# Gated delta-net layer: gram products and decay blocks eight steps ahead, q/k projection nine, nine block buffers, block transfers merged

## The chip, the cores and the metric

One core of one Trainium2 chip (trn2) runs the whole program. The metric is device time in microseconds, the median over runs. All times below are microseconds unless marked ns.

## What is computed

The program is a two-layer transformer on `x` of shape 4 x 256 x 256 (batch `b`, time, width), each layer an attention part and a feed-forward part with adaptive layer norm. The change touches the attention part of the first layer alone, a gated delta rule with 16 key heads and 32 value heads of width 128:

```python
q, k, v = silu(causal_conv4(h @ W_qkvz))      # z is split off before the convolution
q, k = l2norm(q) / sqrt(128), l2norm(k)
def step(S, (q_t, k_t, v_t, a_t, b_t)):       # over 256 times, per batch and value head
    S = S * a_t
    S = S + k_t x ((v_t - S.k_t) * b_t)
    return S, S.q_t
o = rmsnorm(o * silu(z)) * norm_weight        # then @ W_out, gate and residual
```

The recurrence is computed in chunks of 128 times. In each chunk the products k.k and q.k (the gram products), weighted with the decays, give triangular matrices; the lower triangular one has to be inverted.

## The kernel before

**The loop.** The loop over key heads `kh` = 0 to 15 with batches `b` = 0 to 3 inside has 64 steps. All of its order is written out by hand: `pe_step`, `act_step`, `dve_step` and `pool_step` say what TensorE (PE), ScalarE (ACT), VectorE (DVE) and GpSimd (POOL) do in step (kh, b), in this order, and one list of transfers on SyncE (SP) runs beside them. Engines meet at semaphores alone, and each executes its own list in order. Counting the steps as g = 4 kh + b, three kinds of work run ahead of the step that uses them:

- q and k are projected, convolved and squashed eight steps ahead (`LEAD_QK` = 8): `pe_qk`, `act_tap0`, `dve_tap`, `act_silu_qk`.
- The gram products (`pe_gram0`, `pe_gram1`), the decays as scans (`dve_scan`, L843, L846) and their product, the decay blocks `BP` (`dve_scales`, `dve_bp`, L892), are made seven steps ahead (`LEAD_GRAM` = 7). `BP0` and `BP1` hold four batches each, so eight blocks.
- v and z are projected three steps ahead (`LEAD_VZ` = 3).

What runs ahead is done before the loop for the first steps (lists `lead_qk`, `lead_gram`, `lead_taps`, `lead_bp`), and is absent in the last ones.

**The inverses.** The 32 x 32 diagonal blocks of the triangular matrices (64 of them for a head, all batches) go from `BP` to a scratch in DRAM (`sp_blocks_in`, L1076, four transfers for each batch) and from there, one block to a partition, into `Dm` (`sp_blocks_turn`, L1085: eight transfers, for batches 0 to 2 and then for batch 3). POOL inverts them by 31 substitution steps of two instructions (`pool_inverse`, L1023 and L1026) into `Tn`; ACT transposes `Tn` into `Tt` in two halves (`act_turn`, L718, in steps b = 2 and b = 3). `sp_blocks_out` (L1097) writes both to DRAM and `sp_blocks_read` (L1107 for `U`, L1112 for `UT`) brings them back in matrix layout, first for batches 0 and 1, then for 2 and 3. `pe_merge` (L391 to L400, with `act_merge` after each of its four stages) puts the blocks together to inverses of 128 x 128 for two batches in step b = 0 and for the other two in b = 1.

During head kh, POOL inverts the blocks of head kh + 1. `SPLIT` says which of the 31 substitution steps lie ahead of which `pool_ro`:

```python
SPLIT = ((0, 7), (7, 19), (19, 26), (26, BLK - 1))
```

`pool_ro` (L998, a power of four numbers in a partition) is needed at once: `act_ss` (L693) gives the sums of squares of a step's output, `pool_ro` the root, `act_ogn` (L701) the scaled output, `pe_ot` (L444) its transpose, and `pe_f` (L454) the output projection. For b = 0 and b = 1, ACT does all of that in the following step: in `act_step` of (kh, 1), `act_ss` and `act_ogn` of (kh, 0) stand ahead of the first `act_merge`, and in `pe_step` of (kh, 1) `pe_ot` stands ahead of the second `pe_merge` stage.

A step solves with the inverse (`pe_solve`, L420, evicted by `act_y`, L664, twice a step), and multiplies into the output (`pe_o`, L433, L435). In `act_step` of b = 3 the order is the second `act_y`, `act_ots`, and then the second half of `act_turn` for head kh + 1.

Of the kernel before, what the change touches and what calls it, by code (L numbers as in the profile page):

```python
# [23 lines left out]
P = 128  # L24
# [17 lines left out]
MODS = 6  # L42


def build(nc, x_d, wqkvz_d, wba_d, convw_d, dtb_d, alog_d, nw_d, wout_d, wg_d, sg_d, wu_d, su_d, wd_d, sd_d,
# [26 lines left out]
    with outer:  # L72
# [140 lines left out]
        with ExitStack() as s1:  # L213
# [12 lines left out]
            nrm = sb("nrm", [P, B, 4], ctx=s1)  # L226
# [8 lines left out]
            BP = [BP0, sb("BP1", [P, B, 6 * R, P], ctx=s1)]  # L235
            Dm = sb("Dm", [SLOTS, BLK, BLK], ctx=s1)
            Tn = sb("Tn", [SLOTS, BLK, BLK], ctx=s1)
            Tt = sb("Tt", [SLOTS, BLK, BLK], ctx=s1)
# [17 lines left out]
            hact += [BP[1][:].rearrange("p b z t -> p (b z t)")[:, b * 1536:(b + 1) * 1536].rearrange("p (m t) -> p m t", m=HT) for b in range(2)]  # L256

            craw = sb("craw", [B, 2, D], ctx=s1)
            csil = sb("csil", [P, 2, KC, B], ctx=s1)
            wba = sb("wba", [P, KC, NVH * 2], ctx=s1)  # L260
            dtb = sb("dtb", [P, NVH], ctx=s1)
            alog = sb("alog", [P, NVH], ctx=s1)
            ea = sb("ea", [P, NVH], ctx=s1)

            wmod = BP[1][:].rearrange("p b z t -> p (b z t)").rearrange("p (l k n) -> p l k n", l=2, k=KC)
            gx, gn, gu, gw, gl, gd = (Vs[:].rearrange("p b c h d -> p (b c h d)")[:, i * NT * NVH:(i + 1) * NT * NVH]
                                      .rearrange("p (t h) -> p t h", t=NT) for i in range(6))
            alpT = Tt[0:NVH].rearrange("s j i -> s (j i)")
# [16 lines left out]
            LEAD_QK, LEAD_GRAM, LEAD_VZ = 2 * B, 2 * B - 1, 3  # L285
# [79 lines left out]
            def block_of(p, b, h, x, c, i):  # L365

                if c == 0:
                    return BP[p][:, b, (0 if x else 4 * R) + 2 * h + i, :]
                return BP[p][:, b, 2 * R + 2 * h + 1 - x, :]

            def pe_merge(kh, p, g, stage):

                n = 2 * kh + g
                if stage == 0:
                    wait(nc.tensor, "u_zero", 1)
                    wait(nc.tensor, f"t_in0{g}", (kh + 1) * 48)
                    wait(nc.tensor, "og", at(kh, g, 2))
                else:
                    if stage == 1:
                        wait(nc.tensor, f"t_in1{g}", (kh + 1) * 64)  # L380
                    wait(nc.tensor, "u_evac", n * 6 + (1, 4, 5)[stage - 1])
                for i in range(2):
                    b = 2 * g + i
                    for m in range(NC * R):
                        c, h = divmod(m, R)
                        s = i * NC * R + m
                        low = block_of(p, b, h, 1, c, c)
# [15 lines left out]
            def pe_solve(kh, p, b, n):  # L403
# [9 lines left out]
                for h in range(R):  # L413
                    if n == 0:
                        lhs, rhs = UT[:, b, h, :], Vs[:, b, 0, h, :]
                    elif n == 1:
                        lhs, rhs = block_of(p, b, h, 1, 0, 1), Y[:, 0, h, :]
                    else:
                        lhs, rhs = UT[:, b, R + h, :], R2[:, h, :]
# [3 lines left out]
            def pe_o(kh, p, b, c):  # L423
# [7 lines left out]
                for h in range(R):  # L431
                    o = bO[:, (c * R + h) * P:(c * R + h + 1) * P]
                    last = nc.tensor.matmul(o, block_of(p, b, h, 0, 0, c), Y[:, 0, h, :], start=True, stop=(c == 0))  # L433
                    if c == 1:
                        last = nc.tensor.matmul(o, block_of(p, b, h, 0, 1, 1), Y[:, 1, h, :], start=False, stop=True)  # L435
# [432 lines left out]
            def dve_scales(kh, p, b):  # L868
                i = b % 2
                wait(nc.vector, "gram", at(kh, b, 1, 1))  # L870
                wait(nc.vector, "vpow", kh)
                nc.vector.tensor_scalar(nrm[:, b], bG2[:, 256:260], 1e-6, None, ALU.add).then_inc(sem("nrm"), 1)
                wait(nc.vector, "nrm", at(kh, b, 1, 1))
                nc.vector.reciprocal(rcn[i][:], nrm[:, b, 2:4]).then_inc(sem("rcn"), 1)
# [5 lines left out]
            def dve_bp(kh, p, b, c):  # L880
# [4 lines left out]
                for h in range(R):  # L885
                    if c == 0:
                        dst = BP[p][:, b].rearrange("p (z n) t -> p z (n t)", z=3)[:, 0:3:2, 2 * h * P:2 * (h + 1) * P]
                        g, e = bG1[:].rearrange("p (x t) -> p x t", x=2), E1[:, h, :].unsqueeze(1).broadcast_to([P, 2, T])
                    else:
                        dst = BP[p][:, b, 2 * R + 2 * h:2 * R + 2 * (h + 1), :]  # L890
# [99 lines left out]
            def pool_vpow(kh, p):  # L990
                wait(nc.gpsimd, "nrm", (kh + 1) * B)
                wait(nc.gpsimd, "og", (kh - 1) * B * 2)
                nc.gpsimd.tensor_tensor(vsc[p][:], nrm[:], npow[:].unsqueeze(1).broadcast_to([P, B, 4]), ALU.pow).then_inc(sem("vpow"), 1)
# [7 lines left out]
            SPLIT = ((0, 7), (7, 19), (19, 26), (26, BLK - 1))  # L1001
            LAST_SPLIT = ((0, 6), (6, 14), (14, 21), (21, BLK - 1))
# [13 lines left out]
            def pool_inverse(kh, lo, hi):  # L1016

                if lo == 0 and hi > 0:
                    wait(nc.gpsimd, "blk_in", (kh + 1) * 16 * 2 * NBLK)
# [48 lines left out]
            PER_B = NC * R  # L1068

            def sp_blocks_in(kh, b):  # L1070

                wait(nc.sync, "bp", at(kh, b, 4, 4))
                wait(nc.sync, "blk_in", kh * 16 * 2 * NBLK)
                for n in range(NBLK):
                    r = slice(n * BLK, (n + 1) * BLK)
                    nc.sync.dma_start(blkin_dr[n, b].rearrange("c h j i -> j (c h) i"),  # L1076
                                      BP[kh % 2][r, b, 0:4 * R:2, r]).then_inc(sem(f"blk_dr{b}"), 16)

            def sp_blocks_turn(kh, lo, hi):
                for b in range(lo, hi):  # L1080
                    wait(nc.sync, f"blk_dr{b}", (kh + 1) * 16 * NBLK)
                wait(nc.sync, "t_step", kh * NTS)
                for n in range(NBLK):
                    s = slice((n * B + lo) * PER_B, (n * B + hi) * PER_B)
                    nc.sync.dma_start(Dm[s].rearrange("s j i -> s (j i)"),  # L1085
                                      blkin_dr[n, lo:hi].rearrange("b c h j i -> (b c h) (j i)")).then_inc(sem("blk_in"), 16)

            def sp_blocks_out(kh):

                wait(nc.sync, "t_step", (kh + 1) * NTS)  # L1090
                for i, (dr, src) in enumerate(((tinv_dr, Tn), (ttin_dr, Tt))):
                    if i == 1:
                        wait(nc.sync, "t_turned", 2 * (kh + 1))
                    for g in range(2):
                        wait(nc.sync, f"t_in{i}{g}", kh * (48, 64)[i])
# [4 lines left out]
            def sp_blocks_read(kh, g):  # L1100
                bs = slice(2 * g, 2 * g + 2)
                for b in range(2 * g, 2 * g + 2):
                    wait(nc.sync, "y", at(kh - 1, b, 2, 2))
# [905 lines left out]
```

## Time and profile before

| | |
|---|---|
| runs of the program | 1272.46 median, 1269.07 to 1273.2 (3 runs) |
| the profiled execution: span from first to last instruction | 1270.6 |
| busy, share of the span | PE 92%, DVE 72%, ACT 65%, POOL 59% |
| POOL's `vpow` (L993), mean of 16 | 2.9 |
| its mean granted TensorE clock, share of full speed | 0.961 |
| DMA | 143430 packets, 72.82 MB; 116744 packets are under 512 B |

The profiled execution is known by its span; its own time outside the span is not given, and the median of the runs is 1.9 over the span. An engine's busy time counts instructions, not waits. "DMA a<-b" is a transfer, listed under SPq where it is issued; the time shown there is that of the issue. The column "PEclk" of a stretch is the granted TensorE clock (1.00 is 2.4 GHz, 0.50 is 1.2 GHz).

### The profile page before, as it was taken

Reading aid. Unit: us, or ns where it says so; the run is one execution under the profiler, and the core shown is the slowest. Engines: PE = TensorE matmul, PEld = TensorE weight load, DVE = VectorE, ACT = ScalarE, POOL = GpSimd, SP = SyncE. Lnnn points to the kernel's source line nnn. Section 1 sums busy time; section 2 is a strip of 40 time slices with the busy share of each in tenths; the row PEclk is TensorE's granted clock in tenths of the full one; section 3 lists DMA queues with packets and bytes.
Section 4 is the critical chain, followed back from the end, with each engine's and each line's share of the span. In section 5 each row is a group of like instructions: output and inputs, shape, how many; then the busy total and the mean of one; then the engine's idle time right before and its main releaser. Section 6 shows DMA issues by size and latency. Waiting matters only on the chain. (4 is left out here: it accounts for less than half of the span.)

```text
span 1270.6 us, 30469 instructions
## 1 busy us (share of the span) xinstructions
PE 1168.6 (92%) x10744; PEld 1002.5 (79%) x10744; DVE 914.6 (72%) x2304; ACT 831.6 (65%) x2289; POOL 751.5 (59%) x1187
## 2 busy tenths in 40 slices
PE   7787998999999999999999999999998688998986
PEld 6687887888888888888888888888887577776754
DVE  6786787788879797878888888879793414337764
ACT  6334776777777676777777777777675556218973
POOL 3275758586867777776858586858676601104211
PEclk9776999999999999999999999999998979999988
DMA  5212134314040313121222314040214130002000
GB/s 177 64 55 51 66 73 44 83 34 111 7 112 19 99 31 87 37 80 40 80 45 73 65 52 111 6 113 14 62 29 129 25 108 1 1 1 72 2 10 25
DMA packets 143430, 72.82 MB, mean 57 GB/s; under 512 B 116744, under 2 KB 132624, under 8 KB 141360
## 3 DMA queue, kind: packets, MB, share of 16 engines
q1 hardware_dynamic: 143280, 70.89, 22.5%
q8 instruction: 86, 1.41, 0.5%
q14 instruction: 64, 0.52, 0.1%
HBM read 57.06 MB, written 13.78 MB: 56 GB/s over the span
## 5 line engine op out<-in xcount | busy, mean ns | idle before, releaser
L1023 POOL TENSOR_TENSOR tmp<-Dm,Tn 64x31 f32<-64x31 f32 (+15 forms) x496 | 260.5, 525 | 104.0 <-DMA Dm<-blk_in_scratch 69.9
L1026 POOL TENSOR_TENSOR Tn<-Tn,tmp 64x31 f32<-64x31 f32 (+15 forms) x496 | 291.3, 587 | 38.8
L832 DVE SCALAR_TENSOR_TENSOR cv<-bank,cw,cv 128x255 f32<-128x255 f32 (+2 forms) x384 | 155.2, 473 | 145.0 <-ACT cv L631 144.8
L832 DVE SCALAR_TENSOR_TENSOR cqk<-bank,cw,cqk 128x255 f32<-128x255 f32 (+2 forms) x384 | 155.0, 472 | 16.5 <-ACT cqk L631 16.4
L998 POOL TENSOR_TENSOR ro<-ss,mhalf 128x4 f32<-128x4 f32 x64 | 68.0, 1062 | 158.2 <-issue 97.7
L892 DVE SCALAR_TENSOR_TENSOR BP<-bank,cj,E 128x512 f32<-128x512 f32 (+1 forms) x256 | 140.4, 611 | 2.6 <-DVE cj L877 0.3
L454 PE MATMUL bank<-wo,OTs 128*128 128x256 f32 x512 | 132.1, 392 | 0.9 <-ACT OTs L724 0.9
L693 ACT ACTIVATE junk<-og 128x129 f32<-128x129 f32 x256 | 79.6, 311 | 51.6 <-issue 39.4
L701 ACT ACTIVATE ogn<-og,ro 128x128 f32<-128x128 f32 x256 | 81.9, 393 | 44.4 <-POOL ro L998 44.1
L433 PE MATMUL bank<-Y,BP 128*128 128x128 f32 x512 | 95.7, 290 | 7.4 <-ACT Y L664 6.1
L454 PEld LDWEIGHTS bank<-wo,OTs 128*128 128x128 f32 x512 | 91.3, 193 | 12.0 <-ACT OTs L724 1.0
L338 PE MATMUL bank<-hh,wvz_hi 128*128 128x256 f32 x256 | 84.2, 329 | 9.0 <-ACT hT L645 9.0
L433 PEld LDWEIGHTS bank<-Y,BP 128*128 128x128 f32 x512 | 73.0, 193 | 19.4 <-ACT Y L664 19.4
L348 PE MATMUL bank<-wvz_hi,hh 128*128 128x256 f32 x256 | 83.7, 327 | 0.9
L308 PE MATMUL bank<-hh,wqk_hi 128*128 128x256 f32 x256 | 80.4, 314 | 3.1 <-DVE cqk L832 3.1
L664 ACT ACTIVATE Y<-bank 128x256 f32<-128x256 f32 x128 | 48.9, 382 | 51.6 <-PE bank L420 50.5
L318 PE MATMUL bank<-sqk 128*128 128x512 f32 x128 | 67.9, 613 | 8.8 <-DVE BP L892 8.8
L308 PE MATMUL bank<-hh,wqk_lo 128*128 128x256 f32 x256 | 74.8, 292 | 0.0
L308 PE MATMUL bank<-hl,wqk_hi 128*128 128x256 f32 x256 | 74.6, 292 | 0.0
L338 PE MATMUL bank<-hh,wvz_lo 128*128 128x256 f32 x256 | 74.2, 290 | 0.0
L338 PE MATMUL bank<-hl,wvz_hi 128*128 128x256 f32 x256 | 74.0, 289 | 0.0
L348 PE MATMUL bank<-wvz_hi,hl 128*128 128x256 f32 x256 | 73.2, 286 | 0.0
(210 smaller groups left out, 3326.9 us busy)
## 6 DMA issues: line engine op xcount, KB each, us to landing
rvz<-in_L_attn_W_qkvz SPq DMA_DIRECT2D x16, 512.0 KB, 5.5
x<-alpha_scratch SPq DMA_DIRECT2D x8, 1024.0 KB, 6.6
alb<-alpha_scratch SPq DMA_DIRECT2D x7, 1024.0 KB, 6.3
rqk<-in_L_attn_W_qkvz SPq DMA_DIRECT2D x16, 256.0 KB, 2.6
wo<-in_L_attn_W_out SPq DMA_DIRECT2D x16, 256.0 KB, 6.2
blk_in_scratch<-BP SPq DMA_DIRECT2D x256, 16.0 KB, 1.5
tinv_scratch<-Tn SPq DMA_DIRECT2D x32, 128.0 KB, 2.2
tinv_t_scratch<-Tt SPq DMA_DIRECT2D x32, 128.0 KB, 2.2
```

Source lines behind the costliest of these rows:

```text
L308: last = nc.tensor.matmul(bQK[:, t * T:(t + 1) * T], wqk[p][w][:, k, t * DK:(t + 1) * DK], h[:, k, b * T:(b + 1) * T], start=(k + n == 0), ...
L338: last = nc.tensor.matmul(bV[:, t * T:(t + 1) * T], wvz[p][w][:, k, t * DK:(t + 1) * DK], h[:, k, b * T:(b + 1) * T], start=(k + n == 0), ...
L348: last = nc.tensor.matmul(bZ[:, c * 256:(c + 1) * 256], h[:, k, b * T + c * P:b * T + (c + 1) * P], wvz[p][w][:, k, R * DK:2 * R * DK], st ...
L433: last = nc.tensor.matmul(o, block_of(p, b, h, 0, 0, c), Y[:, 0, h, :], start=True, stop=(c == 0))
L454: last = nc.tensor.matmul(bF[:, c * D:(c + 1) * D], OTs[:, h, c, :], wo[p][:, h, :], start=(h == 0), stop=(h == R - 1))
L693: nc.scalar.activation(junk[:], og[b % 2][:, c, h, :], ACT.Square, accum_out=ss[b % 2][:, n:n + 1]).then_inc(sem("ss"), 1)
L701: nc.scalar.activation(ogn[:, c, h, :], og[b % 2][:, c, h, 0:DK], ACT.Copy, scale=ro[b % 2][:, n:n + 1]).then_inc(sem("ogn"), 1)
L832: nc.vector.scalar_tensor_tensor(d, bk[:, t * T:(t + 1) * T - s], cw[p][:, first + t, TAPS - 1 - s:TAPS - s], d, ALU.mult, ALU.add).then_i ...
L892: nc.vector.scalar_tensor_tensor(dst, g, cj[i][:, c, h:h + 1], e, ALU.mult, ALU.mult).then_inc(sem("bp"), 1)
L998: nc.gpsimd.tensor_tensor(ro[b % 2][:], ss[b % 2][:], mhalf[:, 0:4], ALU.pow).then_inc(sem("ro"), 1)
L1023: pool_step_done(nc.gpsimd.tensor_tensor(t, Dm[:, j, j + 1:BLK].unsqueeze(2).broadcast_to([SLOTS, r, c]), Tn[:, j, 0:c].unsqueeze(1).broad ...
L1026: pool_step_done(nc.gpsimd.tensor_tensor(Tn[:, j + 1:BLK, 0:c], Tn[:, j + 1:BLK, 0:c], t, ALU.subtract), kh * NTS + 2 * j + 4)
```

## The change

Steps and buffers: q/k nine steps ahead, gram products and blocks eight, so that one more q/k step and one more gram step lie ahead of the loop. `BP0` holds four blocks and `BP1` five, used in turn. Before the loop, the split of head 2's q/k weights moves ahead of the ninth q/k step. `nrm` gets a second buffer. `Dm` and `Tt` become the halves of one tensor (partitions 0 to 63 and 64 to 127), and some small tensors of the start move into others' space; what those compute is the same.

```diff
+RING = 2 * B + 1
+            BP1 = sb("BP1", [P, RING - B, 6 * R, P], ctx=s1)
+            def bp_of(kh, b):
+                n = (kh * B + b + RING - 1) % RING
+                return BP0[:, n] if n < B else BP1[:, n - B]
-            LEAD_QK, LEAD_GRAM, LEAD_VZ = 2 * B, 2 * B - 1, 3
+            LEAD_QK, LEAD_GRAM, LEAD_VZ = 2 * B + 1, 2 * B, 3
```

POOL: the substitution steps in three parts instead of four; the power `pool_vpow` of the next head behind `pool_ro` of b = 0, not ahead of the inverse; the start of the next inverse (`pool_inverse_start`, L1012, L1013) in b = 3 of the head before.

```diff
-            SPLIT = ((0, 7), (7, 19), (19, 26), (26, BLK - 1))
-            LAST_SPLIT = ((0, 6), (6, 14), (14, 21), (21, BLK - 1))
+            SPLIT = ((0, 15), (15, 25), (25, BLK - 1))
             def pool_step(kh, p, b):
-                if kh + 1 < NKH:
-                    if b == 0:
-                        pool_vpow(kh + 1, 1 - p)
-                        pool_inverse_start(kh + 1)
-                    pool_inverse(kh + 1, *(SPLIT if kh + 2 < NKH else LAST_SPLIT)[b])
+                if b < len(SPLIT) and kh + 1 < NKH:
+                    pool_inverse(kh + 1, *SPLIT[b])
+                if b == B - 1 and kh + 2 < NKH:
+                    pool_inverse_start(kh + 2)
                 pool_ro(kh, p, b)
+                if b == 0 and kh + 1 < NKH:
+                    pool_vpow(kh + 1, 1 - p)
```

SP: one transfer into `Dm` in place of eight, the inverses read for all four batches at once (three transfers for `U` and four for `UT`, twice as large, in place of six and eight), and another order of the list:

```diff
+            def sp_blocks_turn(kh):
+                for b in range(B):
                     wait(nc.sync, f"blk_dr{b}", (kh + 1) * 16 * NBLK)
                 wait(nc.sync, "t_step", kh * NTS)
+                nc.sync.dma_start(Dm.rearrange("s j i -> s (j i)"), blkin_dr.rearrange("n b c h j i -> (n b c h) (j i)")).then_inc(sem("blk_in"), 16)
+            def sp_blocks_read(kh):
+                wait(nc.sync, "y", at(kh, 0, 2))
                 wait(nc.sync, "t_out0", (kh + 1) * 32)
...
                 for kh in range(NKH - 1):
-                    sp_blocks_turn(kh + 1, 0, B - 1)
-                    sp_blocks_in(kh + 1, B - 1)
-                    sp_blocks_turn(kh + 1, B - 1, B)
-                    sp_blocks_read(kh, 1)
+                    ahead = kh + 2 < NKH
+                    if ahead:
+                        sp_blocks_in(kh + 2, 0)
                     if kh + 3 < NKH:
-                        sp_load_qk(kh + 3)
                         sp_load_alb(kh + 3)
-                    if kh + 2 < NKH:
+                    if ahead:
                         sp_load_vz(kh + 2)
                     sp_load_wo(kh + 1)
...
-                    if kh + 2 < NKH:
-                        for b in range(B - 1):
-                            sp_blocks_in(kh + 2, b)
+                    if ahead:
+                        sp_blocks_in(kh + 2, 1)
+                        sp_blocks_in(kh + 2, 2)
+                    if kh + 4 < NKH:
+                        sp_load_qk(kh + 4)
                     sp_blocks_out(kh + 1)
-                    sp_blocks_read(kh + 1, 0)
-                sp_blocks_read(NKH - 1, 1)
+                    if ahead:
+                        sp_blocks_in(kh + 2, B - 1)
+                    sp_blocks_read(kh + 1)
+                    if ahead:
+                        sp_blocks_turn(kh + 2)
```

`sp_blocks_out` is unchanged but for its semaphores: it writes `Tn`, waits until ACT has transposed both halves, and writes `Tt`. `act_step` and `pe_step` are unchanged. Ahead of the loop SP's list ends in `sp_blocks_out(0)`, `sp_blocks_read(0)`, `sp_blocks_in(1, B - 1)`, `sp_load_qk(3)`, `sp_blocks_turn(1)`.

## Rows read from the trace of the kernel before

**Rows 1.** Stretches: heads 1 to 13, head 14, head 15 (start:end, length, PE busy, PEclk, DMA, GB/s)

```profile
167.20:946.00 778.80, 753.32 (x7489) 1.00 0.26 60
946.00:1002.10 56.10, 48.45 (x493) 0.94 0.34 87
1002.10:1067.20 65.10, 50.56 (x461) 0.82 0.22 64
```

**Rows 2.** Stretches: the four steps of head 8, each to the end of its last Y

```profile
588.85:609.54 20.69, 20.06 (x221) 1.00 0.43 90
609.54:626.39 16.85, 16.57 (x200) 1.00 0.32 101
626.39:635.91 9.52, 9.07 (x69) 1.00 0.05 9
635.91:647.98 12.07, 12.04 (x89) 1.00 0.04 7
```

**Rows 3.** Who waited for whom, whole span: us in total, times, longest

```profile
POOL tmp L1023 <- DMA Dm<-blk_in_scratch: 69.9, 16, 7.5
...
ACT ogn L701 <- POOL ro L998: 44.1, 44, 2.5
```

**Rows 4.** Timeline of POOL in head 7: start, us, instruction

```profile
545.81 0.23 POOL L1023 TENSOR_TENSOR tmp<-Dm,Tn 64x31 f32<-64x31 f32 x1 [5.14 <-DMA Dm<-blk_in_scratch]
...
554.16 1.01 POOL L998 TENSOR_TENSOR ro<-ss,mhalf 128x4 f32<-128x4 f32 x1
555.15 0.51 POOL L1023 TENSOR_TENSOR tmp<-Dm,Tn 64x192 f32<-64x192 f32 x1
...
566.20 0.95 POOL L1023 TENSOR_TENSOR tmp<-Dm,Tn 64x256 f32<-64x256 f32 x1
...
582.28 0.44 POOL L1023 TENSOR_TENSOR tmp<-Dm,Tn 64x156 f32<-64x156 f32 x1
```

**Rows 5.** The second step of head 7 as a stretch

```profile
549.12:566.92 17.80, 16.83 (x200) 1.00 0.38 120
```

**Rows 6.** Timeline of ACT at the start of head 8

```profile
588.46 0.39 ACT L664 ACTIVATE Y<-bank 128x256 f32<-128x256 f32 x1
...
589.31 1.11 ACT L718 ACTIVATE Tt<-Tn 64x512 f32<-64x512 f32 x1
...
612.94 0.19 ACT L693 ACTIVATION_READ_ACCUMULATOR junk<-og 128x1 f32 x1
```

**Rows 7.** Timeline of SP's queue, same time: start of issue, us of issuing, transfer, count

```profile
586.09 1.73 SPq L1076 DMA_DIRECT2D blk_in_scratch<-BP  x4
...
590.45 0.77 SPq L1097 DMA_DIRECT2D tinv_t_scratch<-Tt  x2
591.32 1.37 SPq L1107 DMA_DIRECT2D U<-tinv_scratch  x3
593.02 1.78 SPq L1112 DMA_DIRECT2D UT<-tinv_t_scratch  x4
```

**Rows 8.** The page, part 6: KB each, us from issue to landing

```profile
rqk<-in_L_attn_W_qkvz SPq DMA_DIRECT2D x16, 256.0 KB, 2.6
```

**Rows 9.** Stretches: head 14's second step, and the part behind PE's gap

```profile
964.81:983.52 18.71, 15.31 (x177) 0.82 0.66 190
971.25:976.20 4.95, 4.95 (x61) 0.50 0.86 227
```

**Rows 10.** Timelines ahead of the loop: DVE, PE, PE

```profile
102.27 2.19 DVE L892 SCALAR_TENSOR_TENSOR BP<-bank,cj,E 128x512 f32<-128x512 f32 x4
...
104.60 1.10 PE L318 MATMUL bank<-sqk 128*128 128x512 f32 x2 [4.02 <-DVE BP L892]
...
113.79 0.23 PE L391 MATMUL bank<-U,BP 32*32 32x32 f32 x1 [1.92 <-DMA U<-tinv_scratch]
```

**Rows 11.** Timelines near the end of the loop: POOL in head 14, PE in head 15

```profile
968.88 1.01 POOL L998 TENSOR_TENSOR ro<-ss,mhalf 128x4 f32<-128x4 f32 x1
...
1011.74 0.55 PE L338 MATMUL bank<-hh,wvz_hi 128*128 128x256 f32 x1 [5.22 <-ACT hT L645]
```

More of the change, by code:

```diff
@@ L225, in build @@
             sv = [sb(f"sv{i}", [P, R, T], ctx=s1) for i in range(2)]
-            nrm = sb("nrm", [P, B, 4], ctx=s1)
+            nrm = [sb(f"nrm{p}", [P, B, 4], ctx=s1) for p in range(2)]
             ss = [sb(f"ss{i}", [P, 4], ctx=s1) for i in range(2)]
@@ L375, in pe_merge @@
                     wait(nc.tensor, "u_zero", 1)
-                    wait(nc.tensor, f"t_in0{g}", (kh + 1) * 48)
+                    wait(nc.tensor, "t_in0", (kh + 1) * 48)
                     wait(nc.tensor, "og", at(kh, g, 2))
@@ L379, in pe_merge @@
                     if stage == 1:
-                        wait(nc.tensor, f"t_in1{g}", (kh + 1) * 64)
+                        wait(nc.tensor, "t_in1", (kh + 1) * 64)
                     wait(nc.tensor, "u_evac", n * 6 + (1, 4, 5)[stage - 1])
@@ L432, in pe_o @@
                     o = bO[:, (c * R + h) * P:(c * R + h + 1) * P]
-                    last = nc.tensor.matmul(o, block_of(p, b, h, 0, 0, c), Y[:, 0, h, :], start=True, stop=(c == 0))
+                    last = nc.tensor.matmul(o, block_of(kh, b, h, 0, 0, c), Y[:, 0, h, :], start=True, stop=(c == 0))
                     if c == 1:
-                        last = nc.tensor.matmul(o, block_of(p, b, h, 0, 1, 1), Y[:, 1, h, :], start=False, stop=True)
+                        last = nc.tensor.matmul(o, block_of(kh, b, h, 0, 1, 1), Y[:, 1, h, :], start=False, stop=True)
                 last.then_inc(sem("o"), 1)
@@ L870, in dve_scales @@
                 wait(nc.vector, "gram", at(kh, b, 1, 1))
-                wait(nc.vector, "vpow", kh)
-                nc.vector.tensor_scalar(nrm[:, b], bG2[:, 256:260], 1e-6, None, ALU.add).then_inc(sem("nrm"), 1)
+                wait(nc.vector, "vpow", kh - 1)
+                nc.vector.tensor_scalar(nrm[p][:, b], bG2[:, 256:260], 1e-6, None, ALU.add).then_inc(sem("nrm"), 1)
                 wait(nc.vector, "nrm", at(kh, b, 1, 1))
-                nc.vector.reciprocal(rcn[i][:], nrm[:, b, 2:4]).then_inc(sem("rcn"), 1)
+                nc.vector.reciprocal(rcn[i][:], nrm[p][:, b, 2:4]).then_inc(sem("rcn"), 1)
                 wait(nc.vector, "rcn", at(kh, b, 1, 1))
@@ L1018, in pool_inverse @@
                 if lo == 0 and hi > 0:
-                    wait(nc.gpsimd, "blk_in", (kh + 1) * 16 * 2 * NBLK)
+                    wait(nc.gpsimd, "blk_in", (kh + 1) * 16)
                 for j in range(lo, hi):
@@ L1147, in _ @@
                     sp_blocks_in(0, b)
-                sp_blocks_turn(0, 0, B - 1)
-                sp_blocks_turn(0, B - 1, B)
+                sp_blocks_turn(0)
                 sp_load_qk(2)
@@ L1155, in _ @@
                 sp.wait_ge(sem("zero"), 2)
-                sp_blocks_read(0, 0)
+                sp_blocks_read(0)
+                sp_blocks_in(1, B - 1)
+                sp_load_qk(3)
+                sp_blocks_turn(1)
                 def load_ffn():
@@ L1379, in _ @@
                 act.wait_ge(sem("wba_in"), 48)
-                nc.scalar.activation(ea[:], alog[:], ACT.Exp).then_inc(sem("g_act"), 1)
+                nc.scalar.activation(ea, alog, ACT.Exp).then_inc(sem("g_act"), 1)
                 act.wait_ge(sem("g_neg"), 1)
```

89 lines of the change are left out of this document (39 added, 50 removed).

## The prediction

> **What bounds the kernel now.** I began with the page and its busy times: PE 92% of the span, POOL 59%. The chain of waits that ended last covers only the second layer, so the loop has to be read in stretches. Heads 1 to 13 take 778.8, 59.9 a head, and PE is busy for 97% of it at full clock; the last two heads have more idle time, 7.7 in head 14 and 14.5 in head 15 [rows 1]. In a single undisturbed head the four steps take 20.7, 16.85, 9.5 and 12.1, and PE lacks 1.4 in all [rows 2]. So TensorE's own work is the bound, and the change takes none of it away. What it can still do is put waits in or take them out. The list of waits shows where PE is near one: ACT waited 44 times for `ro` of POOL, and POOL 16 times, once for each head, for its blocks in `Dm` [rows 3].
>
> How near, two heads tell. `pool_ro` of step b = 0 can begin when the sums of squares are there, 3.6 after the step's last Y (613.13 - 609.54) [rows 2, 6]. In head 7 POOL was still substituting and began it at 554.16, 5.05 after that Y, and the next step took 17.8 and not 16.85 [rows 2, 4, 5]. `act_ogn` stands ahead of the first `act_merge` on ACT, and PE's transposes and second merge stage wait behind it. So `ro` is free up to 5.05 - 0.95 = 4.1 after the Y, 24.8 after the head's start, and each microsecond later costs one. (All offsets here count from the last Y of the head before, 588.85 in head 8.)
>
> **Part 1: where the inverse starts.** Before, `Dm` was complete at +17.4 in head 7 (545.81 against 528.42), and only seven substitution steps lay ahead of `ro`. Now fifteen do. They take 554.16 - 545.81 = 8.35 for the first seven and 566.20 - 555.15 = 11.05 for the next eight, 19.4 together [rows 4]. To be ready at +24.8 they must start at +5.4. When can they? The new order of SP's list decides:
> - `Tt` cannot be written out before ACT has transposed its second half, and that stands behind the last Y and the `OTs` eviction: 589.31 + 1.11, which is +1.6; SP issues at 590.45 and is done at +2.4 [rows 6, 7].
> - Then come four `sp_blocks_in` of batch 3, ready long before: 1.75 of issuing, to +4.15 [rows 7].
> - Then three reads of `U`, 1.4, and four of `UT`, 1.8 to 1.95 with gaps: +7.55 [rows 7]. I leave the issue times as they are though each read is twice as large, since SP takes 0.43 to 0.46 for 16 KB and for 32 KB alike.
> - Only then `sp_blocks_turn`. One transfer of 256 KB takes 2.6 from issue to landing [rows 8]; the reads ahead of it carry double the packets and are still draining, for which I add an estimate of 0.5. POOL starts at +10.7.
>
> [...]
>
> So `ro` starts at 10.7 + 19.4 = +30.1, 5.3 late. The merges themselves are covered: `U` is asked for at +4.2 and `UT` at +5.6, before they were asked for as late for batches 2 and 3, and the first merge of the head comes after a gram, a q/k and half a v step. If that cover went, it would cost what the reads are late, 1 to 2 a head.
>
> **Part 2: what PE's new gap does to its clock.** A gap of about 5 stands before the transposes once a head, in step b = 1. In head 14 a gap of this kind, 2.95 long, is followed by 4.95 of unbroken PE work at half clock [rows 9]: half of that, 2.5, is the clock's price. Heads 1 to 13 have full clock as a mean [rows 1], so this would be new in each. Bounds: 0 (ACT's evictions may be the slower partner) and 3.5. I take 2.3, just under the row.
>
> **Part 3: the rest of a head.** After `ro` (1.0) POOL does `vpow` (2.9 in the table, now here), ten substitution steps (566.20 to 582.28 less the 1.0 of a `ro` between, 15.1 [rows 4]) and is at +49.1 with the second `ro`. The step's Y is at 37.5 + 5.3 + 2.3 = +45.1, and `ro` is free until about 5 after it. No further delay; the small gap of the third step goes, 0.2. The last six steps and the start of the next inverse fit in what POOL has left. A head is then 59.1 - 0.2 + 5.3 + 2.3 = 66.5, against 59.9 on average: 6.6 x 13 = 86.
>
> **Part 4: ahead of the loop.** One more q/k and gram step. It isn't PE's work (about 3.5, with PE idle there anyway) that counts, but the chain through the engines: PE's last lead gram waited 4.02 for DVE's `BP` [rows 10]. From that `BP` (end 104.46) on: scans of the eighth block 1.9, the moved split 0.7, twelve q/k matmuls at half clock 2.9, ACT 0.8, taps 2.4, scales and `BP` 2.8, in all 11.5 (durations of the same kinds in the timelines there; the `BP` alone is 2.2 [rows 10]). The loop's first gram moves from 104.6 to 116.0. The first merge waited 1.9 for `U` before [rows 10]; the transposes of `Tn` on ACT also move, behind the ninth silu, so that both come at about 123.5. The loop starts 9.5 later. In head 0 the order is the same as in the others: `sp_blocks_turn(1)` stands behind reads, `sp_blocks_in`, and a weight load, POOL starts at about 129, and `ro` is there 6.3 late; with the clock and less 0.3, 8.3.
>
> **Part 5: the end.** The q/k step missing in (13, 3) and the gram missing in (14, 0) are PE time that ends up in gaps of head 14. There `ro` begins 983.5 - 968.9 = 14.6 ahead of the second step's last Y [rows 9, 11]; I keep that, and it now begins at 10.7 + 18.6 = +29.3, which puts the Y at 43.9 against 37.5 (983.5 - 946.0): head 14 is 6.4 longer. Head 15 gains: before, ACT's transposing waited for POOL's last substitution steps with everything behind it, and PE had a gap of 5.2 [rows 11] and a smaller one at its first merge. Now the inverse is done before head 15 and the first merge comes some 6.5 earlier, part of it with a better clock: 8 less.
>
> **Sum.** 9.5 + 8.3 + 86 + 6.4 - 8 = 102. The span of 1270.6 becomes 1373; the median of the runs lies 1.9 over the span, so 1375.
>
> **Rivals.** (1) *Ends faster.* The place is the same, `Dm`'s landing against `ro`; the deciding point is +5.4. If SP's issues overlap so well that POOL starts by then, no head is delayed, the 0.2 to 1.0 of gaps in steps 2 and 3 go (13 x 0.8 = 10), head 14 gains 3, head 15 8, and the start loses 9.5: 1272.5 - 11.5 = 1261. For it: the blocks' data are there 11 earlier than now. Against: the transposing at +1.6 and eleven issues behind it, all seen in the rows. 0.08. (2) *The reads are the next bound.* If SP or the queue needs twice the time for a read of twice the packets, `sp_blocks_turn` goes out at +10.8, POOL starts at +14, and the merge waits too: 8.6 late, clock 3, so 70.5 a head, 10.6 x 14 = 148, and with start and end 1430. For it: some groups of `UT` took 2.9 to 3.5 to issue. 0.08. (3) *It only moves work*: the start's 9.5 and the end's gain cancel because `ro` is absorbed in ACT's idle time: 1272. Against it is head 7's step, which grew by exactly the lateness. 0.03. My forecast has the remaining 0.81.
>
> **How the numbers follow.** A measurement of this kernel can tell about 0.3% (3.8) from no change. In the forecast itself, the start of POOL lies between +9.3 (a landing of 1.9, no tail) and +12.5, fifteen steps between 18.6 and 19.5, the clock between 0 and 3.5: a head between 62.0 and 71. Fourteen heads by that, with a start of 8 to 12 and an end of -10 to +2, give 1300 to 1440; extremes together are unlikely, and rival 2 lies above. For 8 in 10 I take 1315 to 1430. Faster 0.08, same 0.03, slower 0.89.
>
> **What would show it.** Right: SP's one transfer into `Dm` issued about 7.6 after the last Y of a head, POOL's first L1023-type instruction at about +10.7, `ro` of b = 0 starting straight behind the fifteenth substitution step at +30, ACT's `ogn` waiting for it some 5 in every head, a gap in PE before the transposes and PEclk under 1.00 in the stretch of the heads; the first merge near 123 and the gap of 5 at the start of head 15 gone. Wrong: POOL starting by +6, or the second step of a head at 17 as now; then the forecast falls altogether. If the gap is there and PEclk stays at 1.00, only the 2.3 falls, 32 in all.

## The result, and the profile after

The changed kernel takes 1415.2 us in the median of 4 runs (1407.5 to 1430.04), beside 1270.8 for the kernel before on the same chip: a ratio of 1.1105, with an interval of 1.1047 to 1.1163. It is slower by 11%. (Ratios are taken without a run that lies over 1.5% above the fastest of its kernel: here 1430.04, and in experiment 5 one of 1654.74.) The prediction was 1375, between 1315 and 1430, with 0.89 on slower. All times are microseconds. The profiled execution took 1409.8; its span is 1408.0, at a mean granted clock of 0.90 (2.4 GHz is 1.00 and 1.2 GHz is 0.50).

The same three stretches as in [rows 1], first those of the changed kernel:

```profile
184.52:1086.07 901.55, 805.58 (x7477) 0.91 0.21 52
1086.07:1152.86 66.79, 53.01 (x481) 0.82 0.28 73
1152.86:1205.10 52.24, 42.57 (x461) 1.00 0.26 76
```

Heads 1 to 13 take 69.35 each and not 59.91, which is 122.7 more. Head 14 is 10.7 longer, head 15 is 12.9 shorter. Two columns tell more than the length. TensorE's idle time in a head went from (778.80 - 753.32) / 13 = 1.96 to (901.55 - 805.58) / 13 = 7.38, so 5.4 of the 9.4 is new waiting. The other 4.0 is *busy* time, for nearly the same number of matmul records (7477 and 7489): PEclk is 0.91.

The four steps of head 9, to compare with [rows 2] (columns as there):

```profile
736.95:757.65 20.70, 20.12 (x221) 1.00 0.44 107
757.65:783.52 25.87, 19.34 (x200) 0.80 0.13 34
783.52:792.85 9.33, 9.04 (x69) 1.00 0.05 9
792.85:804.90 12.05, 12.02 (x89) 1.00 0.16 45
```

Only step b = 1 changed: 25.87 for 16.85. The third step even lost its small gap (9.33 for 9.52). The wait, as the list of waits for the whole span gives it (us in total, times, longest):

```profile
ACT ogn L707 <- POOL ro L1004: 130.5, 35, 8.9
...
PE bank L450 <- ACT ogn L707: 100.0, 32, 7.2
POOL tmp L1028 <- DMA DT<-blk_in_scratch: 96.3, 16, 9.5
```

ACT's wait for `ro` was 44.1 before [rows 3] and is 130.5. Where it starts is seen in the timelines of head 9. SP's queue (start of issue, us of issuing, transfer, count), then POOL, then PE:

```profile
738.73 0.77 SPq L1097 DMA_DIRECT2D tinv_t_scratch<-DT  x2
739.59 1.82 SPq L1080 DMA_DIRECT2D blk_in_scratch<-BP  x4
741.51 1.44 SPq L1105 DMA_DIRECT2D U<-tinv_scratch  x3
742.99 2.08 SPq L1110 DMA_DIRECT2D UT<-tinv_t_scratch  x4
745.25 0.68 SPq L1087 DMA_DIRECT2D DT<-blk_in_scratch  x1
```

```profile
749.14 0.23 POOL L1028 TENSOR_TENSOR tmp<-DT,Tn 64x31 f32<-64x31 f32 x1 [5.73 <-DMA DT<-blk_in_scratch]
...
767.64 0.67 POOL L1031 TENSOR_TENSOR Tn<-Tn,tmp 64x255 f32<-64x255 f32 x1
768.40 1.01 POOL L1004 TENSOR_TENSOR ro<-ss,mhalf 128x4 f32<-128x4 f32 x1
```

```profile
770.77 1.11 PE L450 MATMUL bank<-eye,ogn 128*128 128x128 f32 x4 [6.36 <-ACT ogn L707]
```

Offsets count again from the last Y of the head before, 736.95. The transfer is issued at +8.3 behind thirteen others, POOL begins at +12.2 (it had been idle for 5.7 just before), fifteen substitution steps take 19.3, `ro` starts at +31.4, and PE pauses for 6.36 before its transposes. The first merge of the loop came at 123.63, against 113.79 [rows 10].

### The profile page after: what moved, and what is told of

Same layout as the page of the kernel before. It is cut to its first block and busy times, and to the rows that moved or that the text cites. A ratio compares the mean times of both kernels' runs of the same rounds, so it can differ in the third digit from the quotient of the medians.

```text
span 1408.0 us, 30196 instructions
## 1 busy us (share of the span) xinstructions
PE 1227.7 (87%) x10744; PEld 1048.5 (74%) x10744; DVE 901.3 (64%) x2304; ACT 835.5 (59%) x2289; POOL 731.9 (52%) x1187
## 5 line engine op out<-in xcount | busy, mean ns | idle before, releaser
L1028 POOL TENSOR_TENSOR tmp<-DT,Tn 64x31 f32<-64x31 f32 (+15 forms) x496 | 253.2, 510 | 131.6 <-DMA DT<-blk_in_scratch 96.3
L1031 POOL TENSOR_TENSOR Tn<-Tn,tmp 64x31 f32<-64x31 f32 (+15 forms) x496 | 281.3, 567 | 38.9
L707 ACT ACTIVATE ogn<-og,ro 128x128 f32<-128x128 f32 x256 | 81.7, 394 | 130.5 <-POOL ro L1004 130.5
L460 PE MATMUL bank<-wo,OTs 128*128 128x256 f32 x512 | 150.2, 432 | 1.3 <-ACT OTs L730 1.3
L450 PE MATMUL bank<-eye,ogn 128*128 128x128 f32 x256 | 47.7, 317 | 100.2 <-ACT ogn L707 100.0
L460 PEld LDWEIGHTS bank<-wo,OTs 128*128 128x128 f32 x512 | 101.9, 215 | 15.3 <-ACT OTs L730 1.6
L450 PEld LDWEIGHTS bank<-eye,ogn 128*128 128x128 f32 x256 | 32.8, 159 | 107.5 <-ACT ogn L707 107.2
L344 PE MATMUL bank<-hh,wvz_hi 128*128 128x256 f32 x256 | 87.3, 341 | 3.1 <-ACT hT L651 3.1
L354 PE MATMUL bank<-wvz_hi,hh 128*128 128x256 f32 x256 | 88.1, 344 | 0.9
L1017 POOL MEMSET Tn<- 64x1024 f32 x16 | 15.1, 945 | 119.3 <-ACT DT L724 119.3
L354 PE MATMUL bank<-wvz_lo,hh 128*128 128x256 f32 x256 | 76.3, 298 | 0.0
```

The lines of the kernel that those rows point to most:

```text
L344: last = nc.tensor.matmul(bV[:, t * T:(t + 1) * T], wvz[p][w][:, k, t * DK:(t + 1) * DK], h[:, k, b * T:(b + 1) * T], start=(k + n == 0), ...
L354: last = nc.tensor.matmul(bZ[:, c * 256:(c + 1) * 256], h[:, k, b * T + c * P:b * T + (c + 1) * P], wvz[p][w][:, k, R * DK:2 * R * DK], st ...
L450: last = nc.tensor.transpose(bOT[:, n * P:(n + 1) * P], ogn[:, c, h, :], ident)
L460: last = nc.tensor.matmul(bF[:, c * D:(c + 1) * D], OTs[:, h, c, :], wo[p][:, h, :], start=(h == 0), stop=(h == R - 1))
L707: nc.scalar.activation(ogn[:, c, h, :], og[b % 2][:, c, h, 0:DK], ACT.Copy, scale=ro[b % 2][:, n:n + 1]).then_inc(sem("ogn"), 1)
L1028: pool_step_done(nc.gpsimd.tensor_tensor(t, Dm[:, j, j + 1:BLK].unsqueeze(2).broadcast_to([SLOTS, r, c]), Tn[:, j, 0:c].unsqueeze(1).broad ...
```

## The experiments

The theory: `ro` of b = 0 queues behind too many substitution steps that begin too late, and the pause that this makes on TensorE costs clock on top. Everything below is measured beside the kernel before. "Half-clock time" is read off one-microsecond stretches of step b = 1.

**1. Nine steps ahead of `ro`.**

```
-            SPLIT = ((0, 15), (15, 25), (25, BLK - 1))
+            SPLIT = ((0, 9), (9, 18), (18, 25), (25, BLK - 1))
```

> The changed kernel with one line altered: GpSimd's substitution split into 9, 9, 7 and 6 steps in place of 15, 10 and 6. Theory (the loss is ro of step b = 0 queued behind 15 substitution steps that can begin only when the one transfer has landed, some 12 us into the head): nine steps from +12.1 end at +22.9, ahead of the sums of squares at +24.3, so ro runs on time at +24.4; step b = 1 returns from 25 to 30 us to 16.9 us, no half-clock stretch is left in heads 1 to 13, a head takes 59.1 us in place of 69.35, and the time is 1415 - 13 x 10.2 - 9.4 (head 0) - 10.7 (head 14) = about 1262 us. First rival (the merged read of the inverses and the one transfer, with their later landings, are themselves what the heads wait for): the split changes nothing of them, heads stay near 69 us, time above 1400. Second rival (POOL is now short of time, since it begins 3 us later than in the kernel before and has the same 31 steps to do): ro is on time but the inverse ends 3 us or more later than +59, the next merge waits, heads of 62 to 63 us, time 1300 to 1320.

Measured: 1279.1, ratio 1.0067 (1.0030 to 1.0104). Heads 2 to 13, head 9's step b = 1, and POOL in that step:

```profile
246.18:957.61 711.43, 692.50 (x6901) 1.00 0.24 61
...
682.45:699.29 16.84, 16.54 (x200) 1.00 0.19 52
```

```profile
686.42 1.01 POOL L1004 TENSOR_TENSOR ro<-ss,mhalf 128x4 f32<-128x4 f32 x1 [1.97 <-issue]
```

POOL now waits for the sums of squares, the step is 16.84 again, and heads 2 to 13 take 59.3 at full clock: 136 of the 144 us are undone by one line. What is late or merged in the transfers is all still there; so neither the merged reads nor the late landing make the loss. They are waited for a little: in some heads the merge waited for `UT`, and step b = 0 took 21.1 in the mean of heads 2 to 13 in place of 20.7. Head 1 (66.9) and head 14 (61.7) kept a half-clock stretch, which I had not expected; with a loop that began 4.3 later than in the changed kernel, they make up the 17 above the 1262 expected.

**2. The transfer early, fifteen steps kept.**

```
@@ sp_blocks_out(kh), between the write-out of Tn and that of Tt
+                        if kh and kh + 1 < NKH:
+                            sp_blocks_turn(kh + 1)
@@ the loop over heads
-                    sp_blocks_out(kh + 1)
                     if ahead:
                         sp_blocks_in(kh + 2, B - 1)
+                    sp_blocks_out(kh + 1)
                     sp_blocks_read(kh + 1)
-                    if ahead:
-                        sp_blocks_turn(kh + 2)
```

> The changed kernel with the split kept at 15, 10 and 6 steps and SyncE's order altered: the blocks of b = 3 are written out ahead of the inverses, and the one transfer back is issued between the write-out of Tn and that of Tt, ahead of the seven reads. Theory (what costs is the start of the substitution at +12 behind SyncE's queue, not the number of steps by itself): the transfer is issued within 1 us of the head's start and lands by about +3.5, ro of b = 3 holds POOL until +6.4, the steps begin at +6.5 in place of +12.1, fifteen of them end at +25.8, ro of b = 0 is 1.4 us late in place of 6.6, step b = 1 takes 18 us, heads 1 to 13 about 60 us, head 0 stays at 69.9, time about 1285 us. Rival (the start of the substitution is set by the transpose of the inverse and the memset behind it, or by the transfer's own 3.4 us meeting the reads): the start stays past +10 and the time over 1380; what the reads lose by being issued 0.5 us later shows as a merge that begins at +9.5 in place of +8.97.

Measured: 1291.3, ratio 1.0194 (1.0155 to 1.0233). SP's queue around the start of head 9 (its zero is 669.71), and that head's step b = 1:

```profile
668.84 0.85 SPq L1099 DMA_DIRECT2D tinv_scratch<-Tn  x2
669.99 0.45 SPq L1087 DMA_DIRECT2D DT<-blk_in_scratch  x1
671.47 0.77 SPq L1099 DMA_DIRECT2D tinv_t_scratch<-DT  x2
```

```profile
690.41:707.75 17.34, 16.77 (x200) 1.00 0.19 51
```

The transfer goes out at +0.3, POOL begins at +6.4 behind the `ro` of b = 3, `ro` of b = 0 starts at +25.3 in place of +31.4, and heads 2 to 12 take 59.6. In these heads each half of the cure takes away nearly all of the loss alone: begin early, or put fewer steps first. The merges still begin at +8.97. Head 0, which the edit leaves alone, kept its pause (7.0), and head 1 took 67.1 with a half-clock stretch of 10.2, where 60 was expected.

**3. The kernel before, with thirteen steps first.**

```
-            SPLIT = ((0, 7), (7, 19), (19, 26), (26, BLK - 1))
+            SPLIT = ((0, 13), (13, 20), (20, 26), (26, BLK - 1))
```

> The kernel before with one line altered: the first part of the substitution 13 steps in place of 7, then 7, 6 and 5. Nothing else of the change is in it: leads, buffers, transfers and reads are the old ones. Theory (the number of steps ahead of ro of b = 0 makes the loss by itself, whatever the leads and buffers): from +15.5 thirteen steps end at about +33.6 (the kernel before shows its thirteenth step's end at +33.5 with one ro between), without that ro at +32, so ro is 7 to 8 us late, step b = 1 takes 25 to 30 us, heads about 70 us, and the time is 1271 + 14 x 10 = about 1400 to 1420 us. Rival (the leads of eight and nine steps or the merged transfers are part of the loss): heads of at most 66 us, time below 1360.

Measured: 1413.5, ratio 1.1165 (1.1102 to 1.1229). Heads 1 to 13:

```profile
177.50:1102.72 925.22, 812.00 (x7489) 0.89 0.22 51
```

71.2 a head, with the old leads, buffers, transfers and reads; `ro` of b = 0 starts at +31.7 to +34.3. A loss of this size in the heads can be made without the rest of the change.

**4. Twelve steps first** (SPLIT of 12, 10 and 9), a dose between.

> The changed kernel with the split 12, 10 and 9 steps in place of 15, 10 and 6: a dose between 9 and 15. Theory (each step ahead of ro costs its own 1.35 us of lateness once POOL ends past +24.4, and the clock's price comes on top with the pause): twelve steps end at +27.2 to +27.4, ro is 2.6 to 3 us late, TensorE pauses 2.4 to 2.8 us, step b = 1 takes 19.5 to 20 us where the clock stays full and 21 to 24 where it is halved; heads of 62 to 66 us, time 1310 to 1360. Rival (the clock's price comes only with pauses of 5 us and more): no half-clock stretch at all, heads of 61.8 us, time about 1303.

Measured in one execution: 1336.4, ratio about 1.05. Heads 1 to 13 take 64.0 in the mean, `ro` of b = 0 began at +26.3 to +28.8. Two steps b = 1, of heads 8 and 10:

```profile
648.07:667.10 19.03, 16.81 (x200) 1.00 0.17 46
...
773.13:798.08 24.95, 22.77 (x200) 0.73 0.13 36
```

Both leave PE idle for 2.2 (length less busy), yet one kept its full clock and the other lost 6 us to it. Over the thirteen heads the half-clock time was 0 once, 3.4 six times and 6.8 to 13.7 six times. The rival falls: small pauses (0.8 to 2.8 here) cost clock too, but not each time.

**5. and 6. The pause filled.** TensorE transposes the identity 18 (then 44) times into the bank that the real transposes overwrite:

```
@@ pe_ot
+                wait(nc.tensor, "vs", min(scaled, 2 * NG))
+                if b == 0 and kh < NKH - 1:
+                    for n in range(18):
+                        nc.tensor.transpose(bOT[:, n % 4 * P:(n % 4 + 1) * P], ident, ident)
                 wait(nc.tensor, "ogn", at(kh, b, 4, 4))
-                wait(nc.tensor, "vs", min(scaled, 2 * NG))
```

> The changed kernel with 18 transposes of the identity added on TensorE in each step b = 1, in the wait for ogn, their results overwritten. They take some 18 x 0.25 = 4.5 us of a wait of 6.4 us and leave ro as late as it is. Theory (beyond the 6.6 us of lateness, step b = 1 loses 2 to 6.4 us because the clock is granted at half after TensorE has stood idle for the wait): with TensorE busy in most of the wait the granted clock stays at its full level in step b = 1, the step takes 16.9 + 6.6 = 23.5 us in every head, heads about 66 us, time 1415 - 14 x 3 = about 1370 us. Rival (the surplus is work that was displaced and runs together, on ScalarE or VectorE, not the clock): the step stays at 25 to 30 us and the time at 1415, or above it where the added transposes push the others back.

Measured: 1409.6, ratio 1.1096 (1.1050 to 1.1143), the same as the changed kernel's within the interval. I had put 0.25 on a transpose; it took 0.12, and the pause stayed at 4.1. That run couldn't decide, so it was repeated with 44:

> As the run with 18 added transposes, with 44. The eighteen shortened TensorE's longest pause in step b = 1 from 6.2 to 4.1 us in the mean over heads 1 to 13 (0.12 us each), and the half-clock time in that step from 13.1 to 8.9 us. Theory (the clock falls because of that pause): 44 x 0.12 = 5.3 us leave a pause of 0.9 us, no half-clock stretch remains, step b = 1 takes 16.9 + 6.3 = 23.2 us in place of 27.2, heads 1 to 13 about 65.3 us, time 1415 - 14 x 4 = about 1360 us, with ro exactly as late as in the changed kernel. Rival (the clock falls for another reason in this step, the added transposes merely shifted it): half-clock time stays near 9 us or more, heads stay at 68 to 69, time 1400 or more.

Measured: 1376.3, ratio 1.0842 (1.0803 to 1.0882). Step b = 1 of head 9, then heads 2 to 13:

```profile
744.58:767.40 22.82, 21.57 (x244) 1.00 0.15 39
...
264.36:1050.70 786.34, 753.60 (x7429) 1.00 0.22 55
```

With added work and `ro` as late as before, heads 2 to 13 take 65.5 in place of 69.5 (65.3 was expected), and PEclk is 1.00 in the mean. `ro` started at +31.2 in the mean of these heads, against +31.4. The 4 us in a head are the clock's, following the pause; one of the twelve heads (head 11) still had a half-clock stretch, of 3.4. The total came out 16 above what I wrote, because head 1 took 76.5 with a half-clock stretch of 17, and the loop began 4 later.

**7. The one transfer in four pieces** of 64 KB, in the same place of the queue.

```
+                for n in range(NBLK):
+                    s = slice(n * SLOTS // NBLK, (n + 1) * SLOTS // NBLK)
+                    nc.sync.dma_start(Dm[s].rearrange("s j i -> s (j i)"),
+                                      blkin_dr[n].rearrange("b c h j i -> (b c h) (j i)")).then_inc(sem("blk_in"), 16)
```

> The changed kernel with the one transfer back of the blocks made as four transfers of 64 KB, issued one behind the other in the same place. Theory (the substitution starts late because the issue stands behind SyncE's seven reads, not because the transfer is one): the start moves by at most 1 us either way from +12.1 (four issues in place of one against shorter transfers), and the time stays within 1% of 1415 us. Rival (the single transfer of 64 partitions is slow by itself, 3.4 us in the median against 2.6 us for rqk of the same size): four pieces land some 1 us earlier, the start falls to +11, heads lose 1 us of lateness each, time about 1395 us.

Measured in one execution: 1421.8, ratio about 1.12. From the page, part 6, of the changed kernel and then of this one (count, KB each, us to landing):

```profile
DT<-blk_in_scratch SPq DMA_DIRECT2D x16, 256.0 KB, 3.4
```

```profile
DT<-blk_in_scratch SPq DMA_DIRECT2D x64, 64.0 KB, 2.2
```

Each piece lands in 2.2, but the last is issued later, and POOL begins between +11.7 and +13.2, at +12.7 in the mean, against +12.2 in the changed kernel. The rival falls: four pieces bring no earlier start. What decides is the place in the queue. Whether the pieces cost something (heads 1 to 13 took 70.4 each, for 69.35) one execution can't tell.

**8. Early transfer and thirteen steps first** (13, 9, 9; in head 0, which still begins late, 9, 9, 7, 6).

> The run with the early transfer, and its substitution split into 13, 9 and 9 steps (9, 9, 7 and 6 in head 0, whose substitution still begins at +15.8). Theory (with the steps begun at +6.4 thirteen of them end at +22.1, two microseconds ahead of the sums of squares, and nine end at about +40.5 ahead of the next): ro is on time in both steps, step b = 1 is 16.9 us in place of 17.35, b = 2 9.3 in place of 9.5, a head 58.95 us in place of 59.58, head 0 60.4 in place of 69.8; head 1 keeps its own stall near +34 and a half-clock stretch (66 to 67 us in both runs so far), head 14 keeps 61.7. From 1291.3: minus 9.4, minus 12 x 0.63, so about 1273 us, level with the kernel before within 0.5%: what the change gains in head 15 it has paid at the start. Rival (the nine steps of the second part end past +41.3 because ro and the power of the norms hold POOL until +28.2): step b = 2 stays at 9.5 or more and the time at 1278 to 1285.

Measured: 1271.4, ratio 0.9989 (0.9967 to 1.0011), level with the kernel before. Heads 2 to 12, then head 1's step b = 1, and PE in it:

```profile
242.30:892.60 650.30, 637.01 (x6337) 1.00 0.25 62
196.23:220.91 24.68, 21.69 (x200) 0.79 0.47 37
```

```profile
207.12 0.18 PE L402 MATMUL bank<-A,UT 32*32 32x32 f32 x1 [1.82 <-issue]
```

```profile
197.35 9.06 SPq L1189 DMA_DIRECT2D gate_scratch<-modT  x8
```

Heads 2 to 12 take 59.1, with `ro` on time; head 1 stands out at 66.8. Its pause has no releaser but "issue", and beside it SP issues eight small write-outs of the gates, the last of these rows.

**9. Those write-outs one to a head, in heads 1 to 8.**

```
-                    if kh == 1:
-                        sp.wait_ge(sem("gates"), 1)
-                        for n in range(4):
-                            for k in range(KC):
+                    if 1 <= kh <= 4 * KC:
+                        if kh == 1:
+                            sp.wait_ge(sem("gates"), 1)
+                        n, k = divmod(kh - 1, KC)
```

> The run with the early transfer and 13, 9 and 9 steps, and the eight small write-outs of the gates, all issued in head 1 so far, issued one to a head in heads 1 to 8. Theory (head 1 loses 7.7 us because those eight transfers keep the DMA engines busy while TensorE and ScalarE pause for issue, 1.8 us at the longest, and the half-clock stretch of 10.2 us follows the pauses): spread, they make no pause above 1 us, head 1 falls from 66.8 to about 59.2 us and no other head grows by more than 0.3 us: 1271 - 7.6 + 1 = about 1264.5 us, 0.5% below the kernel before. Rival (head 1's pause has another source, such as the write-out of the blocks or the loads of weights around it): head 1 stays at 66 to 67 us and the time at 1271.

A miss: 1294.4, ratio 1.0178 (1.0140 to 1.0217). Heads 1 to 8, heads 9 to 12, then PE in head 4:

```profile
177.20:686.40 509.20, 487.24 (x4609) 0.95 0.24 58
686.40:922.50 236.10, 231.47 (x2305) 1.00 0.25 62
```

```profile
391.46 0.28 PE L344 MATMUL bank<-hh,wvz_hi 128*128 128x256 f32 x1 [1.62 <-issue]
```

Head 1 did fall (to 59.9), but heads 2 to 8 rose to between 60 and 65.7, and from head 9 on, without a write-out, a head is 59.0. So the pauses come with the write-outs, and a single one goes with a pause of 0.7 to 2.2 where the eight together made one of 1.8 (3.7 in experiment 1): spreading multiplied the pauses, and the clock's price with them. The theory expected too little of one write-out; the rival falls, since head 1 did follow the write-outs.

**10. The same in the kernel before.**

> The kernel before with the gates' write-outs spread over heads 1 to 8 and nothing else. Theory (the same eight transfers make the 2.8 us pause of head 1, whose step b = 1 takes 20.6 us there): head 1 falls from 64.1 to about 59.9 us, time about 1271 - 4 = 1267 us, so that most of what the spread version of the change gains over the kernel before is the change's own shorter head 15. Rival (the pause has another source): head 1 stays at 64 us, time 1271.

1276.2, ratio 1.0031 (0.9985 to 1.0076): no difference that these runs can tell, and not the 4 of the theory. In its trace head 1 fell to 59.9, as the theory said, and heads 4 to 6 have new pauses of 0.8 to 1.5 at full clock. But the trace is of the shortest of the four executions, 1264.4 at a mean clock of 0.966; the other three took 1272.3 to 1281.6 at 0.952 to 0.958, and what their heads lost isn't on record. So it isn't shown that the write-outs cost the kernel before less than the reordered one.

**11. Experiment 9 with 13 added transposes in heads 14 and 15.**

> The run with the gates' write-outs spread, and 13 transposes of the identity in step b = 1 of heads 14 and 15, in TensorE's wait for ogn (2.6 us in head 14 and 1.6 us in head 15). Theory (the 21.1 us of head 15's step b = 1, against 16.2 in runs in which its clock stays full, and the 3.4 us half-clock stretch of head 14 follow those pauses): the pauses shrink to 1 us and less, head 14 stays at 54 to 55 us, head 15 falls from 57.6 to about 52.7 us, time about 1260 us, 0.8% below the kernel before. Rival (head 15's half-clock stretch follows the turns of the feed-forward weights and their pauses, not the wait for ogn): head 15 stays at 57.6 us, and the time is that of the run with the gates spread, about 1264.5.

1286.9, ratio 1.0125 (1.0094 to 1.0155). The total is off with experiment 9's, on which it was built. Head 15, of experiment 8 and then of this run:

```profile
1005.41:1062.98 57.57, 48.03 (x461) 0.88 0.24 68
```

```profile
1030.04:1082.28 52.24, 44.12 (x474) 1.00 0.26 76
```

Head 15 fell as the theory said, but this doesn't show that the transposes did it: the changed kernel itself and experiment 4 took 52.2 in head 15 without any, with the same pause of 1.56 in step b = 1 and full clock behind it. The other runs with the early transfer (experiments 2, 8, 9) all had the stretch there, so the transposes may have helped. In head 14 the forecast of 54 to 55 was a miss: it took 60.1, with 17.1 at half clock.

**12. The write-outs all behind the loop of heads, 13 transposes in head 15.**

> The run with the early transfer and 13, 9 and 9 steps (level with the kernel before), with the eight write-outs of the gates moved together behind the loop of heads, where SyncE issues them while head 15 runs, and 13 transposes of the identity in step b = 1 of head 15 alone. The run with one write-out to a head has shown a pause in each of heads 1 to 8 and 59.0 us in heads 9 to 13. Theory (each head in which such a write-out is issued behind a step b = 1 pays a pause, and often a half-clock stretch; head 15 pays one pause whatever it holds): head 1 falls from 66.8 to 59.1 us, head 15, 57.6 us there and 52.2 us in the run with transposes added, takes 52 us plus a pause of 1 to 4 us, and the time is 1271.4 - 7.7 - 2 to 5 = about 1260 us, 0.8% below the kernel before. Rival (the write-outs stall head 15, or what follows it, by as much as they did head 1): head 1 falls, head 15 or the stage behind it grows by 6 to 8 us, and the time is 1266 to 1270, level with the kernel before.

Measured: 1268.2, ratio 0.9952 (0.9930 to 0.9975): 0.5% below the kernel before, and the only one of the twelve whose interval lies below 1. Heads 1 to 13, head 15, and PE in head 15:

```profile
179.09:947.80 768.71, 751.50 (x7478) 1.00 0.24 61
1004.06:1067.28 63.22, 49.95 (x474) 0.87 0.43 62
```

```profile
1017.86 0.25 PE L400 MATMUL bank<-UT,A 32*32 32x32 f32 x1 [3.99 <-DMA UT<-tinv_t_scratch]
```

59.1 a head in the mean, head 1 included (59.0). But head 15 is 63.2 and not 53 to 56: the write-outs were issued right behind the reads of `UT`, whose landing the merge now awaited for 3.99 (the last of these reads landed 8.0 after its issue, 2.6 in experiment 8), and a half-clock stretch followed; the first step took 30.0, for 20.1 in experiment 8. That is the rival's case, and the time lies in its range of 1266 to 1270, not at the theory's 1260.

## Why the prediction was right, and where it was off

**The bound and the place: right.** TensorE bounds the loop, the change left its work as it was, and the new wait is `ro` behind fifteen steps behind `Dm`. Experiments 1, 2 and 3 show this from three sides.

**Part 1, a little short.** SP's one transfer was to be issued at +7.55 and went at +8.3 in head 9: the issues ahead of it each took a little longer, the `UT` reads 2.08 for 1.8 to 1.95. From the start of its issue to POOL's first step 3.9 passed; I had 3.15 (2.6 and an estimate of 0.5). POOL began at +11.4 to +12.9 in heads 1 to 13, not +10.7. Fifteen steps took 19.3, 19.4 predicted. The pause on PE was 6.2 in the mean of heads 1 to 13 where I had 5.3. The landing itself was 3.4 in the page of the profile, where I had taken 2.6 from a transfer of weights of the same size [rows 8]. The Trainium skill (DMA: Bandwidth & Descriptors, "Anatomy of one DMA — SWDGE (gpsimd) path") has a fit of about 2.0 plus bytes over 436 GB/s for transfers issued by GpSimd, and these are issued by SyncE; carried over all the same, it gives, as an estimate, 2.6 for this one and 2.15 for a piece of 64 KB. Measured are 3.4 and 2.2 (experiment 7), so it comes out near the pieces and short for the whole.

**Part 2, the term that failed.** "I take 2.3, just under the row", with an upper bound of 3.5. Step b = 1 took 27.2 in the mean: 16.86, plus 6.2 of pause, plus 4.15 of clock. The row I leaned on, head 14's, had 4.95 at half clock behind its gap. In the changed kernel the stretches were 6.8, 10.2 or 17.1 long, counted from their start, which lies in the pause; behind the pause, as in my row, they were 4.8 to 6.1 long in seven heads and 13.2 to 14.4 in six. Heads 7 and 10, their step b = 1:

```profile
622.98:647.69 24.71, 18.81 (x200) 0.86 0.14 36
825.60:854.62 29.02, 22.48 (x200) 0.71 0.12 31
```

The seven paid 2.1 to 2.7, as predicted; the six paid 5.8 to 6.3. In both groups that is 0.44 of the half-clock time behind the pause, so my price for it (one half) was near, and its length was not: one stretch of one head was no bound from above. What makes a stretch short or long stays open. Experiment 6 shows that this is the clock: with the pause filled the surplus went. (My range for a head also had a slip: its terms end at 69.6, not 71. The mean was 69.35, single heads took up to 71.9.)

**Part 3, right in its steps.** `ro` of b = 1 was free, the third step took 9.32 (9.3 predicted), the fourth 12.06. Only the covered merges slipped a little: in some heads `UT` was late and b = 0 took 21.0 to 21.5.

**Part 4, right.** The loop's first gram came at 116.63 (116.0 predicted), the first merge 9.8 later than before (I wrote 9.5, though my own 123.5 makes 9.7), now behind PE's own work and without a wait for `U`. Head 0 took 7.5 more (8.3).

**Part 5, right in direction.** Head 14 grew by 10.7 for 6.4, much of it again the clock (PEclk 0.82, before 0.94): 7.9 came in step b = 1, whose pause was 7.2 for 2.95 and whose half-clock stretch was 17.1 for 6.8. Another 3.1 came in its first step (21.85 for 18.76), which I had put at nothing: PE paused 1.6 there with no releaser but "issue", at a clock of 0.84. Head 15 gained 12.9 for 8: its first step gave 7.8 (27.9 to 20.1), which is what I had worked out, and the second 4.9 only because its half-clock stretch was absent. Experiment 8 has the short first step with the stretch, so that part isn't the change's.

**The sum.** 9.8 + 7.5 + 122.7 + 10.7 - 12.9 = 137.8 (the spans differ by 137.4), against 102. Heads 1 to 13 make up all of the difference: 9.4 a head for 6.6. Of these 2.8, the clock is 1.85, the later `ro` 0.9.

**The rivals.** The second named 70.5 a head and 1430 (its own terms, 148, 9.5 and -8 on 1272.5, make 1422), near the result, by another way (transfer at +10.8, merges waiting); the traces show +8.3 and merges at +8.97, so its number was near by accident. The first, that an early start of POOL would end faster, became experiment 2: begun at +6.4, it removes nearly all of the loss in the heads but not the later start of the loop, 9.8, and with its split adjusted (experiment 8) it ends level. The third, that the lateness is absorbed, is out with the heads themselves, which grew by 9.4 each.

## What to carry to other kernels

A small operation that another engine waits for is as late as what its queue holds ahead of it: before moving a block of work, add the latest time at which it can start to its length, and compare with the time at which that small operation is due; the cure was one line, the split. Price a new pause on TensorE by its length and by the clock behind it, here 6.2 and 4.15 on average, and take the clock's share from several pauses, not one. And a transfer may cost more than its own time, wherever it is put: the eight small write-outs cost head 1 some 8 when issued together (experiment 8), more in all when spread over eight heads (experiment 9), and right behind the reads of `UT` they went with a read that landed late (experiment 12).

## What the runs showed that I had not expected

- In the same step the half-clock stretches were 3.4, 6.8, 10.2, 13.7, 17.1 or 20.5 long, over all runs; pauses of equal idle time (experiment 4) were followed by none or by 13.7. A half-clock microsecond cost about 0.32 (4.15 / 13.1), since 3.7 of a stretch, in the mean of heads 1 to 13 of the changed kernel, lay in the pause itself; behind the pause it cost 0.44.
- A single write-out of the gates, 0.47 of issuing, goes with a pause of 0.7 to 2.2 on TensorE (experiment 9), with no releaser but "issue". What the engine lacks there was not tested.
- The loop's start moves by itself: in the changed kernel and its ten variants the first merge came between 122.3 and 128.1, though the edits left nearly everything ahead of it alone. That is as much as several of the effects above, and a reason to read a head's cost from the heads.
